# Routed front reordered, and the fourth attention item's norm moved up six steps

## The reference

```
x = x + L0_attn(norm(x));  x = x + L0_xattn(norm(x), ctx, gate, mask);  x = x + L0_ffn(norm(x))
x = x + L1_attn(norm(x));  x = x + L1_xattn(norm(x), ctx, mask);        x = x + L1_ffn(norm(x))
...                                       # L2: mixers, then x = x + L2_ffn(norm(x))
...                                       # L3: state space, then x = x + L3_xattn(norm(x), ctx)
# L0_ffn, L1_ffn, L2_ffn: 8 experts, top 1
expert = argmax(xn @ gate)                # one of 8 for each of the 2048 tokens
y = W2[expert] . act(W1[expert] . xn)     # 128 -> 512 -> 128
```

## Time and profile before

| | before |
|---|---|
| median of 3 runs | 1529.95 us (1526.15, 1529.95, 1530.41) |
| profiled execution | 1529.28 us, span 1527.4 us |
| mean granted TensorE clock | 0.869 of 2.4 GHz |
| PE busy | 1186.4 us (78%) |
| DVE busy | 977.2 us (64%) |
| ACT busy | 639.0 us (42%) |
| POOL busy | 596.7 us (39%) |
| DMA | 137.35 MB, mean 90 GB/s |

### The profile page before, as it was taken

How to read it: one execution, slowest core, us unless ns; L and a number is a source line. 1 busy time by engine, 2 the same in 40 slices (tenths; PEclk the granted TensorE clock), 3 DMA queues, 4 the chain that set the end, 5 groups by cost and what they waited for, 6 DMA issues and landing times. The chain is left out here.

```text
span 1527.4 us, 30086 instructions
## 1 busy us (share of the span) xinstructions
PE 1186.4 (78%) x9187; PEld 789.3 (52%) x9187; DVE 977.2 (64%) x4100; ACT 639.0 (42%) x1541; POOL 596.7 (39%) x1132
## 2 busy tenths in 40 slices
PE   3789989998365479999996395884658865999778
PEld 2455555554365245565553294763655642454455
DVE  5777777773566567787772674365655655776445
ACT  2355645444222145666654043330235431666422
POOL 3553478987243344455420443322430112321120
PEclk9699999999578579999998597776787895999889
DMA  6344665530022344455420125001220014341000
GB/s 185 118 129 141 207 183 169 182 122 3 32 60 61 104 127 124 137 168 168 147 82 11 40 57 176 0 15 34 62 76 1 0 39 135 101 123 43 2 0 28
DMA packets 140014, 137.35 MB, mean 90 GB/s; under 512 B 12288, under 2 KB 109184, under 8 KB 139728
## 3 DMA queue, kind: packets, MB, share of 16 engines
q1 hardware_dynamic: 131248, 110.88, 23.9%
q0 software_dynamic: 8608, 24.55, 5.0%
HBM read 83.58 MB, written 49.18 MB: 87 GB/s over the span
## 5 line engine op out<-in xcount | busy, mean ns | idle before, releaser
L762 ACT ACTIVATE L0a_Pr<-PS 128x512 f32<-128x512 f32 (+1 forms) x256 | 136.8, 547 | 137.5 <-PE PS L664 88.4
L762 ACT ACTIVATE L1a_Pr<-PS 128x512 f32<-128x512 f32 (+1 forms) x256 | 136.2, 547 | 100.5 <-PE PS L664 50.5
L479 POOL TENSOR_TENSOR L0a_PG<-L0a_Pr,L0a_G 128x512 f32<-128x512 f32 x80 | 105.7, 1325 | 25.6 <-issue 11.0
L885 DVE CUSTOM_DVE_ANT_0 L1a_junk<-PS,L1a_neg 128x256 bf16<-128x256 f32 x256 | 94.8, 420 | 29.7 <-PE PS L637 29.4
L637 PE MATMUL PS<-L0a_Kst,Qm 128*128 128x256 bf16 (+1 forms) x512 | 94.9, 272 | 16.8 <-DVE L0a_mx L885 9.9
L637 PE MATMUL PS<-L1a_Kst,Qm 128*128 128x256 bf16 (+1 forms) x512 | 94.7, 272 | 16.5 <-DVE L1a_mx L885 9.1
L885 DVE CUSTOM_DVE_ANT_0 L1a_junk<-PS,causal_q 128x128 bf16<-128x128 f32 (+1 forms) x256 | 78.5, 352 | 37.0 <-PE PS L637 36.3
L885 DVE CUSTOM_DVE_ANT_0 L0a_junk<-PS,causal_q 128x128 bf16<-128x128 f32 (+1 forms) x256 | 78.5, 352 | 36.7 <-PE PS L637 36.0
L888 DVE TENSOR_REDUCE L3x_mx<-PS 128x2 f32<-128x512 f32 x128 | 83.8, 685 | 24.5 <-PE PS L637 24.2
L659 PE MATMUL PS<-Qm,L0a_Kst 128*128 128x512 bf16 (+1 forms) x256 | 91.5, 357 | 9.3 <-DMA Qm<-L0a_mT 6.6
L885 DVE CUSTOM_DVE_ANT_0 L0a_junk<-PS,L0a_neg 128x256 bf16<-128x256 f32 x192 | 72.9, 418 | 37.0 <-PE PS L637 36.5
(11 more groups left out here) (739 smaller groups left out, 3183.4 us busy)
## 6 DMA issues: line engine op xcount, KB each, us to landing
Qm<-q_image SPq DMA_DIRECT2D x160, 128.0 KB
sorted_in<-zeros POOLq DMA_DIRECT2D x16, 516.0 KB, 4.3
L0a_Kst<-k_image SPq DMA_DIRECT2D x64, 128.0 KB
ffn_w_<-L_ffn POOLq DMA_DIRECT2D x32, 256.0 KB, 3.5
L1a_Kst<-k_image SPq DMA_DIRECT2D x64, 128.0 KB
ffn_w_<-L_ffn SPq DMA_DIRECT2D x16, 256.0 KB, 6.3
L3x_Kst<-k_image SPq DMA_DIRECT2D x32, 128.0 KB
k_image<-L0a_kpart SPq DMA_DIRECT2D x16, 192.0 KB, 2.6
```

What stands on the lines that cost most here:

```text
L479: g.tensor_tensor(PG[:, V_ % GATED_RING, :].rearrange("p (h q) -> p h q", h=2), Pr[:, V_ % RING, :].rearrange("p (h q) -> p h q", h=2), G[ ...
L762: a(Pr[:, V_ % RING, 0:2 * nq], PS[:, T_BANK + v % 2, 0:2 * nq], ACT.Exp, scale=SCALE)\
L885: ins = v.tensor_tensor_reduce(junk[:, tt, par, 0:nk], scored[:, par], off, 1.0, LOWEST, ALU.add, ALU.max, mx[:, i % 2, tt, par, hp:hp + 1])
```

## The change

In `attention`, the seven steps of the norm (STATS to NORM + 1) get a fourth entry in their lead, 6 slots; XT and XT + 1 keep three entries. The rule that looks a lead up takes the length of the entry. In `experts`, PE's order becomes turn 0, gate 0, turn 1, gate 1, count 0, turn 2, gate 2, count 1, turn 3, gate 3, count 2, count 3; before it was turn 0, turn 1, gate 0, count 0, turn 2, gate 1, count 1, turn 3, gate 2, count 2, gate 3, count 3. On ACT the roots of groups 2 and 3 come before the copies of groups 2 and 3, not 1 and 2, and a copy comes before the second norm of the group before.

```diff
@@ -249,11 +249,12 @@
-    LEAD = {off: (0, 11, 20) for off in (STATS, AGGR, VAR, LN, EXP, NORM, NORM + 1, XT, XT + 1)}
+    LEAD = {off: (0, 11, 20, 6) for off in (STATS, AGGR, VAR, LN, EXP, NORM, NORM + 1)}
+    LEAD.update({off: (0, 11, 20) for off in (XT, XT + 1)})
     LEAD.update({off: (0, 4, 8) for k in (K, Q) for off in range(k, k + 8)})
     def slot_of(i, off):
-        return PER * i + off - (LEAD[off][i] if i < 3 and off in LEAD else 0)
+        return PER * i + off - (LEAD[off][i] if off in LEAD and i < len(LEAD[off]) else 0)
     def at(n, off):
         return next((i for i in range(N) if slot_of(i, off) == n), None)
@@ -1045,7 +1046,7 @@
         blocks_out = lambda k, n: 16 * ((nth - 1) * len(range(k, BLOCKS, YS_RING)) + n)
-        ROOTS_FIRST = ((0, 1), (2,), (3,), ())
+        ROOTS_BESIDE = ((0, 1), (), (2,), (3,))
         def registers(tile, a, b, engine, top):
             return nc.values_load_multi_w_load_instructions(tile[0:1, a:b], engines=(engine,), min_val=0, max_val=top,
@@ -1127,12 +1128,12 @@
                                  start=False, stop=True, **free)
                     ins.then_inc(s["cum_psum"], 1)
-                for g in range(NQ + 1):
-                    if g < NQ:
-                        turn_group(g)
+                for g in range(NQ):
+                    turn_group(g)
+                    gate_group(g)
                     if g >= 1:
-                        gate_group(g - 1)
                         count_group(g - 1)
+                count_group(NQ - 1)
                 pe.wait_ge(s["sofar_ready"], NQ)
                 mm(PS[:, GATE_BANK, 0:E], core.ones_b[:, :], sofar[:, NQ - 1, :], start=True, stop=True, **free)\
                     .then_inc(s["tot_psum"], 1)
@@ -1198,11 +1199,11 @@
                     ins.then_inc(s["row_ready"], 1)
                 for g in range(NQ):
-                    for n in ROOTS_FIRST[g]:
+                    for n in ROOTS_BESIDE[g]:
                         root(n)
+                    act_copy(core, act, xT[:, g * QT * P:(g + 1) * QT * P], PS[:, XT_BANK + g, :], s["xT_psum"], g + 1, s["xT_ready"])
                     if two_norms and g > 0:
                         second_norm(g - 1)
-                    act_copy(core, act, xT[:, g * QT * P:(g + 1) * QT * P], PS[:, XT_BANK + g, :], s["xT_psum"], g + 1, s["xT_ready"])
                 if two_norms:
                     second_norm(NQ - 1)
                 act.wait_ge(s["plan_ready"], len(STEPS) + 1)
```

## The result

| | before | after |
|---|---|---|
| median, same session | 1525.36 us (1522.5 to 1530.41, 6 runs) | 1516.3 us (1512.75 to 1520.62, 6 runs) |
| ratio, 95% interval | | 0.9936 [0.9914, 0.9959] |
| profiled execution, its span | 1529.28, 1527.4 us | 1520.62, 1518.8 us |
| mean granted TensorE clock | 0.869 | 0.871 |
| PE, DVE, ACT, POOL busy | 1186.4, 977.2, 639.0, 596.7 us | 1187.3, 977.1, 640.3, 597.9 us |

What follows compares the result with a forecast made beforehand. Bound by chains of waits between engines: gates and scatters in the fronts, norm and SyncE's queue in attention. 3.3 + 2.8 + 2.8 + 1.9 + 1.3 - 0.5 = 11.6 us, from 1529.95 to 1518.3 us; range 1512.2 to 1524.2.

Steps and rivals of the forecast that it cites:

- the three terms 3.3, 2.8, 2.8: Fronts of L0f, L1f, L2f: third scatter batch starts earlier by 3.3, 2.8 and 2.8 us.
- If the scatters did not bound, the gain would be 4.2: L0f's front: place 3 comes 4.2 us earlier, the whole gain if GpSimd's scatters did not bound; used for the range's lower end.
- the 1.1 us per front that I left out: Fronts: given back if all last eight scatter issues took the longest, 8 x 0.14 us; not counted.
- the up to 3.3 us that I had worked out: Fronts: by the skill's rule of GpSimd and VectorE sharing SBUF interfaces, the sum would be up to 3.3 us less.
- Root 2 "costs nothing": L0f's front: root 2, due at 399.4, is reached by ScalarE at about 399.3, so moving it costs nothing.
- The norm 3.1 us earlier: L0a: fourth item's norm ready at 42.05 instead of 45.13, its GpSimd operations now before the third item's q cut.
- the q parts 0.6 late: L0a: third item's q parts come 1.6 us later; their DMA starts at 45.25 instead of 44.62, 0.6 late.
- Gains: 1.9 and 1.3: L0a and L1a: maxima go at 53.8 and 544.6 instead of 55.69 and 545.91, gaining 1.9 and 1.3 us.
- The queue has 2.43 and 1.78 us of slack: SyncE's queue before the maxima, L0a and L1a; argued against the rival that only the fronts count.
- L3x "+0.5": L3x: first row maximum at 1283.2 instead of 1282.25, 0.4 comes back; cost 0.5 us, bounds 0 and 0.9.
- only the fronts count: Rival: late q eats the early norm's gain, L3x costs 0.9; 8.0 us, 1522.0 us; chance 0.16.
- SyncE's queue does not hold: Rival: attention groups L0a and L1a give all of their 3.1; 15.1 us in all, 1514.9 us; chance 0.12.

Runs made afterwards that it cites:

- ScalarE issuing: Whole change, with the first item's maxima DMAs issued by ScalarE behind its copy instead of by SyncE behind the loads; 0.996 of before.
- the weights late: Kernel before plus early norm, with GpSimd issuing the next network's first weights DMA (256 KB) six slots later; 0.9993 of before, 1522.76 us.
- the split: Second half of the third item's loads issued behind the maxima: early norm with old fronts 0.9962, 1517.46 us; whole change 0.9901, 1507.83 us.

## Why the prediction was right or wrong
- **What bounds the fronts, and the three terms 3.3, 2.8, 2.8: right,** place by place in L0f (3.35, 2.9 and 2.8 in the distances), and alone they are the measured gain (0.9943 is 8.7 us of 1524, with 9.0 in the distances of that run).
- **"If the scatters did not bound, the gain would be 4.2":** they do. The third batch is 3.3 earlier, the last eight are as far apart as before, and the fetch is 3.3 earlier. The scatters' issue did not slow (962 ns in the median, 958 before), so the 1.1 us per front that I left out was rightly left out. The Trainium skill, GPSIMD Engine Reference, section 8, has VectorE and GpSimd contend for shared SBUF interfaces; the up to 3.3 us that I had worked out for that do not show.
- **Root 2 "costs nothing":** right in place, but the edit on ScalarE is more than that. I treated it as a detail; it is the half without which the other loses 12 us.
- **The norm 3.1 us earlier, the stall at slot 10 about 1 us, the q parts 0.6 late, the maxima right behind the loads: right** (42.07, 1.76 and 1.37, 45.22 against 44.62, 54.83 and 542.75). In L0a 54.83 is 1.0 later than the 53.8 of the working, since two load issues took 2.21 us instead of 1.20. They do so in each kernel with the early norm and all eight loads ahead in L0a (1.95 to 2.21), with ScalarE issuing and with the weights late too; why stays open.
- **"Gains: 1.9 and 1.3": wrong, and this is the step that failed.** I let the landing follow the issue at the distance of before, and wrote "no DMA moves". One did: with its norm work done earlier, GpSimd issued the 256 KB of weights ahead of the maxima (54.25 and 541.62) instead of behind them. Beside that and the loads the landing took 5.5 and 6.5 us, not at most 4.2 and 4.7, and the two gains came out as 0.4 and 0.6 us lost. With the weights late it took 4.7 in both, and slot 24 stood 1.3 and 2.6 us earlier than before: together 3.9, near the forecast 3.2, though the time of that run doesn't show it. "The queue has 2.43 and 1.78 us of slack" was true of the issue and said nothing of the landing. What I wrote against the rival was its weak point.
- **The total.** 9.8 us against 11.6 is near only because the terms that failed are 3.2 of the 11.6 and the measurement can't tell 2 us; the distances add up to 8.2.
- **L3x "+0.5": mis-sized.** The first row maximum came 0.8 later, slot 24 not at all (49.5 against 49.6).
- **The rivals.** The result is that of *only the fronts count* (8.0 us; -9.1 + 0.4 + 0.6 - 0.1 = -8.2 by the distances), by another mechanism than the late q that I gave it: with q as late as with the change, the split brings the gain back. *SyncE's queue does not hold* is out. The mean clock hardly moved (0.869, 0.871), so neither of the clock's rivals is needed.

## What to carry to other kernels
A slack read between two issues on a queue is no slack for the landing. A small transfer that someone waits for can be late twice: in its issue, behind bulky loads on the same queue, and in its landing, when other engines put out traffic beside it. So put the bulky loads behind it if their own users are later, and when an engine gets time back, ask which DMA it will now issue sooner. When two waits end close together, removing one may show nothing; remove each alone and both together (slot 24 of L0a here: 0 to 0.3 us later with either, 2.7 earlier with both). And when an order is changed on two engines, cost each half alone: one of them may be a loss that only the other repays.

## What had not been expected
- 64 KB for which TensorE waits took 3.9 to 4.9 us from issue to use in L0a and L1a when the second half of the loads was out of the way, 4.7 with all eight loads (128 KB each) ahead and the weights late, 5.5 to 6.5 with both ahead, and 7.0 to 7.2 from ScalarE beside both. A DMA share of 0.8 went with landings of 4.7 us and of 5.5 us alike.
- The early norm let GpSimd come to the weights' DMA earlier, from 3.2 us behind the maxima's issue in L0a to 0.6 ahead of it (58.89 and 55.69; 54.25 and 54.83); issuing it six slots later won 1.6 and 1.8 us at slot 24.
- With the loads split and the norm early the granted clock, averaged over each kernel's runs, was 0.877 to 0.878, against 0.873 in the runs of before beside them. Whether that is a part of the gain or only goes with it, no run here tells.
